# Graph network kernel: the first layer's node rows computed beside its hops, and the sums added to them by accumulating scatters

## The reference, cut to what matters

```python
h = jnp.maximum(_layernorm(x, axis=-1), 0.0)
x = x + _L0_gnn_ref(edge_index, h)

def _L0_gnn_ref(edge_index, embedding_weight):
    row, col = (edge_index[0], edge_index[1])
    deg = jax.ops.segment_sum(jnp.ones_like(row, ...), row, num_segments=n)
    deg_inv_sqrt = jnp.where(deg > 0, jax.lax.rsqrt(jnp.maximum(deg, 1.0)), 0.0)
    x = embedding_weight
    acc = x
    for _ in range(NUM_LAYERS):            # three hops
        m = deg_inv_sqrt[row][:, None] * x[col]
        x = jax.ops.segment_sum(m, row, num_segments=n) * deg_inv_sqrt[:, None]
        acc = acc + x
    return acc / (NUM_LAYERS + 1)
```

## Time and profile before

| | us |
|---|---|
| median of three runs | 10337.89 (10337.08 to 10356.35) |
| the profiled execution, its own time | 10289.74 |
| its span, from the first to the last instruction | 10287.9 |
| busy in it: PE, DVE, ACT, POOL | 6857.5, 5347.9, 3591.8, 6746.0 |

### The profile page before, as it was taken

How to read it: one execution, slowest core, us unless ns; L and a number is a source line. 1 busy time by engine, 2 the same in 40 slices (tenths; PEclk the granted TensorE clock), 3 DMA queues, 4 the chain that set the end, 5 groups by cost and what they waited for, 6 DMA issues and landing times. The chain is left out here.

```text
span 10287.9 us, 118581 instructions
## 1 busy us (share of the span) xinstructions
PE 6857.5 (67%) x25794; PEld 5061.5 (49%) x25794; DVE 5347.9 (52%) x21331; ACT 3591.8 (35%) x11394; POOL 6746.0 (66%) x6677
## 2 busy tenths in 40 slices
PE   7699786518889544400888816889896288989900
PEld 4355443217667433300666615767674176777700
DVE  9799898514422111155555556767666766222210
ACT  0011111014411000055555656767676576111100
POOL 7777777777567777701776606767674276767677
PEclk9899999755555555555555555555555555555555
DMA  4222212256466222243222336867655677785511
GB/s 138 58 55 48 50 20 50 62 79 147 115 91 105 54 48 48 44 169 144 71 72 71 74 88 112 118 110 123 105 95 102 142 119 111 99 98 77 75 38 40
DMA packets 1491536, 890.23 MB, mean 87 GB/s; under 512 B 1261101, under 2 KB 1299049, under 8 KB 1490949
## 3 DMA queue, kind: packets, MB, share of 16 engines
q0 software_dynamic: 213248, 189.76, 20.9%
q1 hardware_dynamic: 601112, 499.16, 17.0%
q10 hardware_dynamic: 676716, 196.73, 8.0%
HBM read 603.97 MB, written 286.87 MB: 87 GB/s over the span
## 5 line engine op out<-in xcount | busy, mean ns | idle before, releaser
L1383 POOL DMA_INDIRECT work<-table,work x3136 | 3128.5, 998 | 1850.3 <-DVE work L1412 905.1
L957 PE MATMUL bank<-work 128*128 128x64 f32 x7056 | 2422.6, 447 | 1374.3 <-DMA work<-table,work 1028.0
L960 PE MATMUL bank<-work 32*128 32x64 f32 x7820 | 2679.0, 444 | 204.4 <-ACT work L969 201.7
L957 PEld LDWEIGHTS bank<-work 128*128 128x128 f32 x7056 | 1765.2, 310 | 1800.6 <-issue 1411.0
L960 PEld LDWEIGHTS bank<-work 32*128 32x128 f32 x7820 | 1943.9, 306 | 675.7 <-ACT work L969 232.5
L969 ACT ACTIVATE work<-bank 32x64 f32<-32x64 f32 x3920 | 854.8, 218 | 3281.5 <-PE bank L960 2911.3
L302 ACT ACTIVATE work<-work 128x64 f32<-128x64 f32 x4704 | 1799.0, 432 | 94.8 <-DVE work L293 39.8
L1673 POOL DMA_INDIRECT acc<-x,work x784 | 761.9, 972 | 751.6 <-DVE work L1776 527.2
L1412 DVE TENSOR_SCALAR work<-end_idx 128x7 int32 (+1 forms) x464 | 93.6, 203 | 1956.8 <-DMA work<-table,work 1953.8
L638 POOL DMA_INDIRECT acc<-node_tab,acc x784 | 767.1, 978 | 258.2 <-issue 258.2
L269 DVE BATCH_NORM_STATS2 work<-work 128x6 f32<-128x64 f32 x4704 | 634.8, 211 | 419.3 <-ACT work L302 381.9
(11 more groups left out here) (164 smaller groups left out, 8449.0 us busy)
## 6 DMA issues: line engine op xcount, KB each, us to landing
work<-skey SPq DMA_DIRECT2D x560, 448.0 KB, 4.7
table<-work ACTq DMA_DIRECT2D x336, 224.0 KB, 3.5
work<-table,work POOLq DMA_INDIRECT x3136
work<-xd SPq DMA_DIRECT2D x84, 448.0 KB, 3.9
z<-zeros ACTq DMA_DIRECT2D x64, 392.0 KB, 5.4
work<-lowrow SPq DMA_DIRECT2D x196, 128.0 KB, 2.9
acc<-in_x SPq DMA_DIRECT2D x28, 896.0 KB, 4.5
acc<-z SPq DMA_DIRECT2D x28, 896.0 KB, 6.3
```

Of the source, the lines that this page charges most:

```text
L957: ins = nc.tensor.matmul(o, sel[:, k, :], rows[:, k, :], start=True, stop=not before)
L960: ins = nc.tensor.matmul(o, self.join[b % 2][:, k, :], self.inn[(b + k + 1) % 2], start=False, stop=True)
L1383: nc.gpsimd.indirect_dma_start(got[b % NB][:, k, :], None, source, bass.IndirectOffsetOnAxis(ap=gidx[b % NB][:, k:k + 1], axis=0)).then_in ...
```

## The change

The buffer z0 and the phase `nodes_after_first` are gone. x1 gets E spare rows behind its NP node rows. The second and the third hop each take 28 half chunks (14 rows per partition) of x, do layer norm and ReLU, and store x + h / 4 into x1: `load_base` on SP in every even group, `base_stats` at the end of VectorE's even groups, `bln.root`, `bln.shift` and two rows per tile in the odd groups (`base_rows` on ScalarE), `base_sum` on VectorE in the next even group, `store_base` on ScalarE's queue in the next odd group. The third hop's `post` scales `acc` in place by a quarter of 1/degree. When all gathers of that hop are issued and all stores of base rows have landed, POOL issues 392 scatters that add the rows of `acc` to x1 in memory; an edge that isn't a node's last has the number of its own spare row, so that no bounds check is used. The spare rows are filled with zeros by 32 stores. In all eight hops POOL's list is unrolled, and it reads its indices directly from `end_idx` (or `scat_idx`), without the copies of `stage`.

```diff
-        z0 = dram("z0", [NP, C])
-        x1 = dram("x1", [NP, C])
+        x1 = dram("x1", [NP + E, C])
+        spare = sb("spare", [P, T], I32)
...
+                    nc.gpsimd.iota(spare[:], [[P, T]], base=NP, channel_multiplier=1).then_inc(s_iota, 1)
...
-                    z = z0.rearrange("(p c) d -> p (c d)", p=P)
-                    for k in range(C):
+                    z = x1[NP:NP + E, :].rearrange("(p c) d -> p (c d)", p=P)
+                    for k in range(T * C // NC):
                         act.dma_start(z[:, k * NC:(k + 1) * NC], zeros[:]).then_inc(s_clear, 16)
...
-                c.do(nc.vector.tensor_copy(scat_idx[:, a, 0:T], m[:, :, 0]))
+                if a:
+                    c.do(nc.vector.tensor_copy(scat_idx[:, a, 0:T], m[:, :, 0]))
+                else:
+                    own = m[:, :, 2]
+                    c.do(nc.vector.tensor_copy(own, spare[:]))
+                    c.wait()
+                    c.do(nc.vector.tensor_tensor(own, own, skey_col[:, a, :], ALU.subtract))
+                    c.wait()
+                    c.do(nc.vector.tensor_scalar(m[:, :, 0], m[:, :, 0], SKIP, None, ALU.is_ge))
+                    c.wait()
+                    c.do(nc.vector.tensor_tensor(own, own, m[:, :, 0], ALU.mult))
+                    c.wait()
+                    c.do(nc.vector.tensor_tensor(scat_idx[:, a, 0:T], own, skey_col[:, a, :], ALU.add))
...
+            if base is not None:
+                bcur, bh = [take(DH, C) for _ in range(2)], take(DH, C)
+                bln = Norm("nb", DH)
+                vx, v1b = (t.rearrange("(p j c) d -> j p c d", p=P, c=DH) for t in (x, x1[0:NP, :]))
+                first_chunk = base * (NG // 2)
...
+                    def load_base(i, m):
+                        f = m % 2
+                        if reused(i, m, 2):
+                            sp.wait_ge(s_bst[f], i * 32 + m // 2 * 16)
+                        sp.dma_start(bcur[f], vx[i * 4 + (m + first_chunk)]).then_inc(s_bin[f], 16)
...
                         load_keys(sp, a, g, kr[b % 2], s_kr[b % 2])
                         sums.load(sp, i, b, g)
+                        if base is not None and b % 2 == 0:
+                            load_base(i, b // 2)
...
+                    def store_base(i, m):
+                        act.wait_ge(s_bdone, i * 4 + (m + 1))
+                        act.dma_start(v1b[i * 4 + (m + first_chunk)], bcur[m % 2]).then_inc(s_bst[m % 2], 16)
+                    def base_rows(i, b, k):
+                        m = b // 2
+                        if k == 0:
+                            bln.root(act, i * 4 + m)
+                            if reused(i, m, 1):
+                                if m:
+                                    store_base(i, m - 1)
+                                else:
+                                    store_base(i - 1, 3)
+                        if k == 0 and reused(i, m, 1):
+                            act.wait_ge(s_bdone, i * 4 + m)
+                        bln.apply(act, bcur[m % 2], bh, ACT.Relu, i * 4 + m, range(2 * k, 2 * k + 2))
                     def group(i, b, g):
                         for k in range(G):
                             sums.hand_on(act, i, b, g, k)
+                            if base is not None and b % 2:
+                                base_rows(i, b, k)
...
-                    groups(pool, gather)
+                    for g in range(NG):
+                        b = g % NB
+                        if g >= NB:
+                            wait_apart(pool, passed, sums.summed(g - (NB - 1)))
+                        for k in range(G):
+                            t = g * G + k
+                            nc.gpsimd.indirect_dma_start(
+                                got[b][:, k, :], None, source,
+                                bass.IndirectOffsetOnAxis(ap=idx[:, t:t + 1], axis=0)
+                            ).then_inc(got_in[b].sem, 16)
                     if to_nodes is not None:
+                        for f in range(2):
+                            pool.wait_ge(s_bst[f], 16 * (NG // 4))
+                        for g in range(NG):
+                            pool.wait_ge(s_scat, g + 1)
+                            for k in range(G):
+                                t = g * G + k
+                                nc.gpsimd.indirect_dma_start(
+                                    to_nodes, bass.IndirectOffsetOnAxis(ap=scat_idx[:, a, t:t + 1], axis=0),
+                                    acc[:, t, :], None, compute_op=ALU.add).then_inc(put_out.sem, 16)
+                        pool.wait_ge(put_out.sem, put_out.end)
...
-                            nc.vector.tensor_tensor(tb[b2], acc[:, cols, :], bcast(rdeg[:, a, cols], C), ALU.mult
-                                                    ).then_inc(s_scat, 1)
+                            nc.vector.scalar_tensor_tensor(acc[:, cols, :], acc[:, cols, :], 0.25,
+                                                           bcast(rdeg[:, a, cols], C), ALU.mult, ALU.mult
+                                                           ).then_inc(s_scat, 1)
+                    def base_stats(i, m):
+                        f, n = m % 2, i * 4 + m
+                        dve.wait_ge(s_bin[f], i * 32 + (m // 2 * 16 + 16))
+                        bln.stats(Chain(dve, s_bdve, n * Norm.STEPS), bcur[f], n)
+                    def base_sum(i, m):
+                        bln.done(dve, i * 4 + m)
+                        nc.vector.scalar_tensor_tensor(bcur[m % 2], bh, 0.25, bcur[m % 2], ALU.mult, ALU.add
+                                                       ).then_inc(s_bdone, 1)
...
                             rows_in(i, b)
-                            stage(g + 2, b + 2)
+                            if base is not None and b % 2:
+                                bln.shift(dve, i * 4 + b // 2)
+                            if base is not None and b % 2 == 0 and (b or later(i)):
+                                if b:
+                                    base_sum(i, b // 2 - 1)
+                                else:
+                                    base_sum(i - 1, 3)
...
                                 post(i - 1, TURN - 1, g - 1)
+                            if base is not None and b % 2 == 0:
+                                base_stats(i, b // 2)
...
-        hop(0, table[0], end_idx[:, 0, :], to_table=table[1], ordered=1)
-        hop(0, table[1], end_idx[:, 0, :], to_nodes=z0)
-        nodes_after_first()
+        hop(0, table[0], end_idx[:, 0, :], to_table=table[1], ordered=1, base=0)
+        hop(0, table[1], end_idx[:, 0, :], to_nodes=x1, base=1)
```

More of the change, by code:

```diff
@@ L365, in _ @@
                 def _(dve):
-                    dve.wait_ge(s_iota, 2)
+                    dve.wait_ge(s_iota, 3)
                     nc.vector.tensor_copy(steps16[:], whole)
@@ L462, in _ @@
                     act.dma_start(node_tab.rearrange("(p c) f -> p c f", p=P), tab).then_inc(s_out, 16)
-                    act.wait_ge(s_clear, 16 * C)
+                    act.wait_ge(s_clear, 16 * (T * C // NC))
                     act.wait_ge(s_out, 16)
@@ L1225, in _, with hop @@
                     dve.wait_ge(s_acc, 2 * NG)
-        def hop(a, source, idx, to_table=None, to_nodes=None, dense=None, ordered=None):
+        def hop(a, source, idx, to_table=None, to_nodes=None, dense=None, ordered=None, base=None):
             ph.next()
@@ L1231, in hop @@
             s_st = [ph.sem(f"h_st{b}") for b in range(2)]
-            put_out = [ph.landed(f"put{b}", 16 * G * (NG // 2) if to_nodes is not None else 0) for b in range(2)]
-            s_stage, s_sel, s_tab, s_acc, s_scat, s_sidx = (
-                ph.sem(n) for n in ("h_stage", "h_sel", "h_tab", "h_acc", "h_scat", "h_sidx"))
+            put_out = ph.landed("put_nodes", 16 * T if to_nodes is not None else 0)
+            s_sel, s_tab, s_acc, s_scat, s_bdone, s_bdve = (
+                ph.sem(n) for n in ("h_sel", "h_tab", "h_acc", "h_scat", "b_done", "b_dve"))
+            s_bin, s_bst = ([ph.sem(f"{n}{f}") for f in range(2)] for n in ("b_in", "b_st"))
             s_nin, s_nfree, s_ndone, s_nout, s_ndve = (
@@ L1238, in hop @@
             got = [take(G, C) for _ in range(NB)]
-            gidx = [take(G, dt=I32) for _ in range(NB)]
             kr = [take(G, P) for _ in range(2)]
@@ L1242, in hop @@
             tb = [take(G, C) for _ in range(2)]
-            sidx = [take(G, dt=I32) for _ in range(2)]
             sums = Sums("h", a, [(2 * b, 2 * b + 1) for b in range(NB)])
+            if base is not None:
[3 more added lines that the diff above has]
+                first_chunk = base * (NG // 2)
             order = Order(ordered) if ordered is not None else None
@@ L1249, in hop @@
                 gb, bb = (t[:].unsqueeze(1).to_broadcast([P, DH, C]) for t in (gamma_b, beta_b))
-                v1, vo = ([t[:, :, f * DH:(f + 1) * DH, :] for f in range(2)] for t in node_chunks()[2:])
```

(22 more changed lines are left out.)

70 lines of the change are left out of this document (removed).

## The result

In one set of runs the changed kernel took 10208.42 us (median of 4, 10161.33 to 10220.51), the kernel before 10337.49 (4, 10330.11 to 10356.35): ratio 0.9868 [0.9849, 0.9886], 129 us less where 443 were forecast, and outside the range of 9850 to 10110. Both kernels took longer in the first set, the changed one by 105 us, the one before by 44; what of that could be explained stands with the last experiments.

The account below looks back on a forecast made before the run. GpSimd bounds the third hop, GpSimd and TensorE tie in the second, and the node pass stands alone. -437.6 + 8 + 8 - 13 - 12 + 3.5 = -443 us from 10289.7 gives 9847, plus 48 is 9895; range 9850 to 10110.

Parts of the forecast that it names:

- the price of an accumulating scatter: Third hop, GpSimd: 0.98 us each, with idling 1.287, so 392 scatters take 504 us; third hop +8 us in all.
- upper end of 1.47: Third hop: GpSimd's us per accumulating scatter, half as much again, if each row needs two reads and one write described.
- The argument for the low end: Third hop: gathers at 0.94, scatters at 0.969 and 0.982 us differ by 4%, so an accumulating scatter was taken as 0.98.
- Rival 1: Third hop: accumulating costs GpSimd more, each row being read once more; at 1.5 times 0.98, +192 us, 10087; chance 0.17.
- Rival 2: Third hop: accumulating transfers don't overlap, 4.4 us per scatter, 1219 us added, 11114, so slower; chance 0.07.
- Node pass: Pass over node rows after the third hop: it goes, its barrier included, -437.6 us.
- Seam: Third hop: landing, last group, post, base_sum and store between last gather and first scatter, about 18 us.
- Gathers of the third hop: 502 us at the second hop's mean plus 14 for stretching beside VectorE's two-input base_sum.
- Second hop: Base work for chunks 0 to 27: +13 for ScalarE less 5 of stage waits, +8 us, bounds -5 and +40.
- ScalarE's hand-overs: Second hop: first tile of each odd group exposed, about 1.7 against 1.23 us, 28 x 0.45 = 13 us.
- Rival 3: Second and third hop: base rows don't hide, loads and stores late or hand-overs pushed; 9959, or +56 us; chance 0.12.
- Later hops: Six later hops without index staging: -13 us from earlier first gathers, -12 from GpSimd's waits inside.

Follow-up runs that it names:

- the last experiments: Repeat runs of both kernels, and the changed kernel with gathers of a group waiting until the group two before landed: throttled 10080.18 and 10088.83 us.
- before_again: The kernel before, unchanged, run once more with a profile: 10289.87 us.
- after_again: The changed kernel itself, run again in a later set on one other chip: 10103.8 us against 10293.02 for the kernel before, ratio 0.9814.
- plain_scatter: The changed kernel with the third hop's 392 scatters writing over the base rows instead of adding: 9873.02 us in a single run.
- before_unstaged: The kernel before without index copies and with gathers unrolled in the seven hops that scatter nothing: 10275.99 us against 10292.16, ratio 0.9978.
- no_base_rows: The changed kernel without base-row work in the second and third hop, x copied to x1 in an earlier stage: 10056.02 us in a single run.
- half_accumulate: The changed kernel with the first 196 accumulating scatters cut to 64 of 128 rows, the last 196 to 32 of 64 numbers: 10075.37 us.
- half_plain: half_accumulate with its halved scatters writing instead of accumulating: 9857.04 us in one run.
- after_third: The changed kernel once more, with a profile: 10065.6 us.

## Why the prediction was wrong, point by point

By stages, before_again to after_again: node pass -438, third hop +255, second hop +17, later hops -19, all other stages -1: -186, and the spans differ by 185.9.

- **The failed step is the price of an accumulating scatter**, taken as 0.98 us from the nearest row, since gathers and scatters "differ by 4% though they do different things". It is 1.561, above even the upper end of 1.47. The list was forecast as 504 us and took 4688.95 - 3942.55 = 746; with the plain price it took 508. This term alone is 242 of the 257 us between forecast (-443) and after_again (-186); plain_scatter, which takes only the accumulation away, shows that it is this step. The argument for the low end compared two transfers that each only copy; it said nothing of a third kind. And of 392 equal instructions the price was the only one no row showed, so the range had to carry it, with a ceiling that was itself a guess of what is written per row: the price turned out to be mostly per transfer.
- **Rival 1** was the right one in kind, time of GpSimd in each scatter, at 1.59 times instead of 1.5; its reason, that each row is read once more, is not what the price goes by, since half the rows leave 0.50 of the added 0.59 us. **Rival 2** is out: landing is 3.2 us against 2.2, yet one is issued each 1.90, and all transfers fill 0.32 of the stretch. The Trainium skill's "DMA: Bandwidth & Descriptors", section "Rules for kernel authors", says that an accumulate reads its destination and writes it later; a landing that takes 1 us longer agrees with that, but it was hidden.
- **Node pass**: -438, as forecast. **Seam**: 19.05 against 18. **Gathers of the third hop**: 3923.5 - 3400.3 = 523 against 516.
- **Second hop**: +17 (552 to 569) against +8, inside its bounds, but for another reason than given. Without staging the hop takes 548 (before_unstaged) to 544 us (no_base_rows) in place of 552, so 4 to 8 came back (5 forecast); the base rows cost 25, for the most part not through ScalarE's hand-overs (13 forecast) but because GpSimd paces this hop and VectorE's two-input operations stretch its gathers (19.3). That effect was counted in the third hop and left out here. The Trainium skill's "SBUF — State Buffer", section "Who interferes with whom", infers that such operations don't hold up descriptor writing; the 19.3 us speak against the inference for indirect transfers.
- **Rival 3** (base rows don't hide): 25 + 27 us in both hops, 8.3 + 19.3 of it stretching, 18.8 seam, most of it priced. The transfers of base rows were about as quick as taken (4.4 us), even in the first profile; KB each, median us to landing:

```profile
work<-in_x SPq DMA_DIRECT2D x56, 448.0 KB, 4.8
...
x<-work ACTq DMA_DIRECT2D x56, 448.0 KB, 2.9
```

- **Later hops**: -19 in both other executions (3267 against 3286) where -25 was forecast, and -16 for unstaging alone, over seven hops. The +68 of the first profile goes with that execution's slow transfers.
- **Small slips of the sums** change nothing: 392 x 1.23 is 482 and not 484 us, 0.98 + 0.305 is 1.285 and not 1.287, and six hops of 0 to 12 us make 0 to 72, not 22 to 66; 12 was taken.

## What to carry to other kernels

An operation that the trace doesn't show must not be priced like its nearest neighbour when it is issued 392 times on the engine that paces the stage; measure it by itself first, or let the range reach to where it decides. A transfer that replaces arithmetic moves the work to the engine that issues it: here the accumulation, 0.59 us per 128 rows, gave back 237 of the 438 us won. And work put "beside" a hop is priced on the engine that paces this hop, not on the engine that does it.

## What the runs showed of the hardware

- An accumulating indirect scatter of 128 rows of 256 bytes costs GpSimd 1.561 us, a plain one 0.971. Accumulating also sends more packets: the page counts 257,152 in that queue where plain_scatter has 213,248, which is 392 x 112 more. A plain indirect transfer has 32 of them (213,248 for 6664 transfers), an accumulating one 144. half_accumulate has 31,360 more than half_plain, 196 x (48 + 112). This fits one packet per row in place of 16 on one side of the transfer (64 - 16 = 48, 128 - 16 = 112), which is inferred from the counts. The time does not follow that count: the added 48 packets go with 0.50 us, the added 112 with 0.59.
- Gathers were stretched by operations of VectorE with two inputs in memory (one from 0.94 to 1.51 us beside base_sum), not by the statistics with one (0.94 to 0.95 us), in the rows of after_again.
- The stage `tables` took 412 us in the changed kernel's first profile and 377 in after_third, the same kernel; its gathers of line 453 then took 1021 instead of 1307 ns each:

```profile
L453 POOL DMA_INDIRECT work<-in_x,dst_idx x252 | 329.4, 1307 | 89.3 <-issue 76.5 <-remote 12.9
```

```profile
L453 POOL DMA_INDIRECT work<-in_x,dst_idx x252 | 257.2, 1021 | 89.2 <-issue 76.5 <-remote 12.7
```

The first is the changed kernel's first profile, the second after_third's. A difference of some 35 us between single executions can therefore be this stage, and no effect of an edit.
